# A dense mixture of experts, worked row by row only for the chosen experts, in two halves of the tokens

## The reference

```python
x = _layernorm(x + attention(x))        # 16 heads of 128, causal
x = _layernorm(x + _L0_ffn_ref(x))      # 32 experts of width 96, top 6 by sigmoid, shared width 192
x = _layernorm(x + _L1_attn_ref(x))     # a state space model (SSM), 8 heads, causal convolution, gated
x = _layernorm(x + _L1_ffn_ref(x))      # 16 experts of width 176 in 4 groups (2 groups, then top 4), shared width 352
```

## Time and profile before

| what | value |
|---|---|
| time, median of 3 runs | 1664.05 us (1663.39 to 1666.93) |
| profiled execution: its own time and its span | 1664.1 us, the same, as the time counts from the first to the last instruction |
| instructions | 29632 |
| PE busy | 1607.4 us, 97% |
| DVE, ACT, POOL busy | 1131.1, 764.6, 628.7 us |
| DMA moved | 277.75 MB, mean 167 GB/s |

### The profile page before, as it was taken

How to read it: one execution, slowest core, us unless ns; L and a number is a source line. 1 busy time by engine, 2 the same in 40 slices (tenths; PEclk the granted TensorE clock), 3 DMA queues, 4 the chain that set the end, 5 groups by cost and what they waited for, 6 DMA issues and landing times.

```text
span 1664.1 us, 29632 instructions
## 1 busy us (share of the span) xinstructions
PE 1607.4 (97%) x9944; PEld 1403.7 (84%) x9944; DVE 1131.1 (68%) x2877; ACT 764.6 (46%) x1889; POOL 628.7 (38%) x379
## 2 busy tenths in 40 slices
PE   7999999999999979999999999999999999999997
PEld 6988888898888868888888888888888888888886
DVE  5878878787887765556467568748784867753533
ACT  5666656666665543434433443325333533323221
POOL 2322223232222004323377335841575147533242
PEclk9999999999999999999999999999999999999999
DMA  6444335343443016666676556655655466555563
GB/s 212 159 140 143 141 118 180 132 158 139 142 141 137 1 59 205 191 196 205 199 225 188 184 176 209 194 187 165 207 189 175 146 206 197 178 175 172 195 206 107
DMA packets 101241, 277.75 MB, mean 167 GB/s; under 512 B 13488, under 2 KB 17584, under 8 KB 100112
## 3 DMA queue, kind: packets, MB, share of 16 engines
q1 hardware_dynamic: 101136, 276.39, 51.6%
HBM read 229.18 MB, written 46.63 MB: 166 GB/s over the span
## 4 chain that ended last, share of the span: by engine, by line
PE 60%; issue 14%; DVE 13%; POOL 6%; ACT 4%; DMA 1%; SPq 1%; POOLq 0%; DVEq 0%; ACTq 0%
PE psum L352 54%; POOL act_sb L578 4%; PE psum L1324 2%; DVE s_sb L1019 1%; PE psum L1335 1%; PE psum L1514 1%; POOL mix L600 1%; ACT p_sb L701 1%; PE psum L1314 1%; ACT kT_hi L660 1%; DVE s_sb L1017 1%; DVE kT_lo L913 1%; DVE pT_lo L1034 1%; DVE x L934 1%; DVE p_sb L1027 1%
## 5 line engine op out<-in xcount | busy, mean ns | idle before, releaser
L352 PE MATMUL psum<-xT_hi,gu_w 128*128 128x512 f32 x1616 | 550.3, 401 | 4.2 <-DVE act_sb L1082 4.0
L578 POOL TENSOR_TENSOR act_sb<-act_sb,comb 128x512 f32<-128x512 f32 x184 | 311.1, 1691 | 614.8 <-DVE act_sb L1082 614.6
L1082 DVE TENSOR_TENSOR act_sb<-psum,gated 128x512 f32<-128x512 f32 x204 | 140.7, 690 | 378.9 <-PE psum L352 372.6
L742 ACT ACTIVATE gated<-psum 128x512 f32<-128x512 f32 x204 | 122.2, 599 | 600.3 <-PE psum L352 597.8
L352 PEld LDWEIGHTS psum<-xT_hi,gu_w 128*128 128x128 f32 x1616 | 304.2, 188 | 78.0 <-DVE act_sb L1082 5.6
L352 PE MATMUL psum<-xT_lo,gu_w 128*128 128x512 f32 x808 | 319.6, 395 | 0.0
L352 PEld LDWEIGHTS psum<-d_w,act_hi 128*128 128x128 f32 x1632 | 221.5, 188 | 19.7 <-issue 2.1
L544 POOL TENSOR_TENSOR split_stage<-raw_stage,split_stage 128x768 fp32r<-128x768 f32 x56 | 103.1, 1840 | 354.2 <-ACT split_stage L650 354.2
L352 PE MATMUL psum<-d_w,act_hi 128*128 128x256 f32 x1632 | 227.7, 282 | 0.4 <-ACT act_hi L750 0.4
L352 PEld LDWEIGHTS psum<-xT_lo,gu_w 128*128 128x128 f32 x808 | 152.2, 188 | 28.8
L1088 DVE TENSOR_TENSOR act_lo<-act_sb,act_hi 128x512 fp32r<-128x512 f32 x204 | 148.8, 729 | 2.1 <-ACT act_hi L750 1.8
(11 more groups left out here) (203 smaller groups left out, 3473.6 us busy)
## 6 DMA issues: line engine op xcount, KB each, us to landing
gu_w<-w_split SPq DMA_DIRECT2D x204, 512.0 KB, 3.6
d_w<-w_split SPq DMA_DIRECT2D x204, 256.0 KB, 3.8
w_split<-split_stage SPq DMA_DIRECT2D x56, 768.0 KB, 3.9
raw_stage<-w_all SPq DMA_DIRECT2D x56, 384.0 KB, 4.3
decay_all<-decay_dram SPq DMA_DIRECT2D x32, 384.0 KB, 5.3
in_w<-w_split SPq DMA_DIRECT2D x40, 256.0 KB, 4.1
aw_raw<-attn_w SPq DMA_DIRECT2D x8, 1024.0 KB, 6.3
comb<-l_comb_dram SPq DMA_DIRECT2D x128, 64.0 KB, 3.1
```

The source lines that it names most:

```text
L352: last = nc.tensor.matmul(out_ap, w, m, start=start and n == 0, stop=stop and n == len(pairs) - 1, **kw)
L578: pool.tensor_tensor(act_sb[:, s % 2, :], act_sb[:, s % 2, :], comb[:, comb_block(s) % 2, :], ALU.mult).then_inc(comb_done, 1)
L742: act.activation(gated[to, s % 2, :], psum[0:to.stop - to.start, G_BANK, :], ACT.Silu).then_inc(gated_ready, 1)
L1082: dve.tensor_tensor(act_sb[r, s % 2, :], psum[r, G_BANK if packed(s) else U_BANK, :], gated[r, s % 2, :], ALU.mult).then_inc(t_ready, 1)
```

## The change

Attention stays as it is, without the splitting of weights for later layers. In its place SP zeroes two areas in DRAM (`xs`, one for each half of the tokens, 42 stores).

The feed-forward layers work only chosen rows. Tokens are taken in two halves of 1024. After the norm, DVE chooses experts per token (`choose`), and a place is made for each (token, chosen expert): PE counts with a triangular matrix (`rank`), DVE makes row numbers (`slots`), and POOL scatters each token's row to them, one indirect DMA of 128 rows for each tile and choice (`scatter`). Every expert has its own region of 1024 rows in `xs`. A block is 128 consecutive rows of one region. The number of blocks is fixed by the worst case: 79 per half in the first layer, 47 in the second. `table` makes, on DVE, the first row of each block; SP reads it into registers (8 at a time) and loads the block's weights and rows by it (`block_load`). PE turns the rows (`block_turn`), makes gate and up and down (`block_gate_up`, `block_down`), ACT does the silu, DVE the product (`block_act`), ACT copies the result out, SP stores it. POOL gathers for each token its 6 or 4 result rows (`gather`), and DVE adds them to x with their weights (`combine`). All of this, the shared blocks and the SSM are multiplied in plain fp32, one matmul for a product, no split.

The stream (`STREAM`) has 316 blocks: 16 shared blocks of the first layer (two for each tile of 128 tokens, half 0), 79 chosen of half 0 with the 16 shared ones of half 1 placed in pairs after each 8, 79 chosen of half 1, then in the second layer 16 shared and 47 chosen for each half. The SSM's parts for half 0 are spread over the blocks of the first layer's half 1 (90 slots over 79 blocks), those for half 1 over the second layer's shared and chosen blocks of half 0 (90 slots over 63). `slots_at` gives the slots behind a block. The second layer's half 1 and the last gathers have no SSM beside them.

```diff
-L0 = dict(layer=0, experts=32, width=96, shared=192, top=6, rows=32, reuse=3)
-L1 = dict(layer=1, experts=16, width=176, shared=352, top=4, groups=4, top_groups=2, rows=16, reuse=11)
+HALVES = 2
+HALF_TILES = TILES // HALVES
+HALF_T = T // HALVES
+BLOCK = 128
+L0 = dict(layer=0, experts=32, width=96, top=6, up=2 * 96)
+L1 = dict(layer=1, experts=16, width=176, top=4, groups=4, top_groups=2, up=3 * P)
...
+def most_blocks(f):
+
+    return (HALF_T * f["top"] + f["experts"] * (BLOCK - 1)) // BLOCK
...
+BETWEEN = 8
+STREAM = shared_blocks(L0, range(HALF_TILES))
+FIRST = {}
+for _f, _h in ((L0, 0), (L0, 1), (L1, 0), (L1, 1)):
+    if _f is L1:
+        FIRST["shared", _h] = len(STREAM)
+        STREAM += shared_blocks(L1, range(HALF_TILES * _h, HALF_TILES * (_h + 1)))
+    FIRST[_f["layer"], _h] = len(STREAM)
+    for _m, _b in enumerate(routed_blocks(_f, _h)):
+        STREAM.append(_b)
+        if (_f, _h) == (L0, 0) and _m % BETWEEN == BETWEEN - 1 and _m < HALF_TILES * BETWEEN:
+            STREAM += shared_blocks(L0, [HALF_TILES + _m // BETWEEN])
...
+XB_RING, OUT_RING = 4, 4
+L1_RING = 4
+L0_RING = 2 * L1_RING
...
+FRONT = 8, 40
+SLOTS = 90
+SPAN = (FIRST[0, 1], FIRST["shared", 0]), (FIRST["shared", 0], FIRST["shared", 1])
+
+
+def slots_at(n):
+
+    for h, (a, b) in enumerate(SPAN):
+        if a <= n < b:
+            for v in range((n - a) * SLOTS // (b - a), (n - a + 1) * SLOTS // (b - a)):
+                yield h, v
...
+            def block_load(n):
+                f, h, m, _ = STREAM[n]
+                r = ROUTED_OF[n]
+                row = first_row_of(n)
+                k, turn = ring_of(r)
+                if r < L0_ROUTED:
+                    if r >= L0_RING:
+                        sp.wait_ge(b_down_done, ROUTED[r - L0_RING] + 1)
+                else:
+                    sp.wait_ge(b_down_done, ROUTED[max(r - L1_RING, L0_ROUTED - 1)] + 1)
...
+            for n in range(-4, BLOCKS + 1):
+                for lead, f in ((4, L0), (3, L1)):
+                    if 0 <= n + lead < BLOCKS and is_routed(n + lead) and STREAM[n + lead][0] is f:
+                        block_load(n + lead)
+                if n >= 1 and is_routed(n - 1):
+                    block_store(n - 1)
...
+            def scatter(f, q):
...
+                for t in range(QUAD * q, QUAD * (q + 1)):
+                    for k in range(f["top"]):
+                        pool.indirect_dma_start(xs[q // 2], bass.IndirectOffsetOnAxis(ap=row_of[:, t, k:k + 1], axis=0), x[:, t, :], None) \
+                            .then_inc(scattered[q], 16)
...
+            def combine(f, t):
...
+                dve.wait_ge(og_loaded[i % MIX_RING], 16 * gathered(f, t))
+                for k in range(f["top"]):
+                    ins = dve.scalar_tensor_tensor(x[:, t, :], og[:, i % MIX_RING, k, :], mix_of[f["layer"]][:, t, k:k + 1], x[:, t, :], ALU.mult, ALU.add)
...
             def project(p, k):
-                n, part = IN_JOBS * p + k, slice(p * PT, (p + 1) * PT)
-                pe.wait_ge(in_loaded[n % IN_RING], 16 * (n // IN_RING) + 16)
-                pairs = []
-                for c in range(DC):
-                    w = slice(c * P, (c + 1) * P)
-                    pairs += passes(in_w[:, n % IN_RING, 0, w], in_w[:, n % IN_RING, 1, w], xT_hi[:, c, part], xT_lo[:, c, part])
-                chain(psum[:, proj_bank(k), :], pairs).then_inc(proj_ready, 1)
+                part = slice(p * PT, (p + 1) * PT)
+                chain(psum[:, proj_bank(k), :], [(in_w[:, k, c, :], xT[:, c, part]) for c in range(DC)]).then_inc(proj_ready, 1)
...
+            block_gate_up(0)
+            for n in range(BLOCKS):
+                if n + 2 < BLOCKS and is_routed(n + 2):
+                    block_turn(n + 2)
+                if n + 1 < BLOCKS:
+                    block_gate_up(n + 1)
+                block_down(n)
```

More of the change, by code:

```diff
@@ new lines, with out_place, ring_of @@
+L0_ROUTED = HALVES * L0["blocks"]
+XB_RING, OUT_RING = 4, 4
+L1_RING = 4
+L0_RING = 2 * L1_RING
+def out_place(n):
+    f, h, m, _ = STREAM[n]
+    before = sum(-(-STREAM[FIRST[k]][0]["blocks"] // 2) for k in ((0, 0), (0, 1), (1, 0), (1, 1)) if FIRST[k] < FIRST[f["layer"], h])
+    return before + m // 2, m % 2
+def ring_of(r):
+    if r < L0_ROUTED:
+        return r % L0_RING, r // L0_RING
+    r -= L0_ROUTED
+    k = r % L1_RING
+    return k, len(range(k, L0_ROUTED, L0_RING)) + r // L1_RING
@@ new lines, in gathered @@
+def gathered(f, t):
+    return sum(LAYERS[i]["top"] for i in range(2) for u in range(TILES)
+               if (i, u) <= (f["layer"], t) and (i * TILES + u) % 2 == (f["layer"] * TILES + t) % 2)
+FRONT = 8, 40
[6 more added lines that the diff above has]
+                yield h, v
```

1483 lines of the change are left out of this document (734 added, 749 removed).

## The result

The changed kernel took 1996.82 us (1992.68 to 2003.11, 4 runs) against 1663.80 (1663.39 to 1666.93) for the one before on the same chip: ratio 1.199 [1.197, 1.202]. The forecast was 1740 (1590 to 1870): the sign was right, the size much too small. Later, beside other kernels, the same unedited kernel took 2011 and 1995, but once 1867.5 (ratio 1.120 [1.117, 1.122]). So 129 us of the 257 by which the forecast was short come and go from one set of runs to another, and 128 are always there. Both need a cause.

The account below looks back on a forecast made before the run. PE was taken as the bound, busy 97% of the span. Attention 612, then the start, four feed-forward stages and tail summed to 1714; on 1102 us, the accounting's 3% shortfall added 30: about 1740 us, range 1590 to 1870.

Parts of the forecast that it names:

- Start of the stream: After attention (612): 48 POOL scatters 1.0 us apart from about 600 to 650, first chosen block at 655, bounds 636 and 690.
- second rival: Scatters and gathers: POOL's DMAs take 1.7 us, lengthening start, both span starts, second-pair products and tail; 1870 us, chance 0.12.
- First layer, half 0: 79 chosen and 16 shared blocks: PE 148 us, DVE's weight bursts +25, loads hardly above PE's pace; 176 us, to 831.
- The two stages with the SSM: First layer half 1 takes 291 us, to 1122; second layer half 0 takes 327, to 1449.
- Larger-of sum: SSM stages: each block costs the larger of PE's and DVE's time, summed block by block: 277 and 295 us.
- 6 us a tile against a slot of 3: Start of first layer's half 1: sums wait for six gathers a tile, 6 us against a slot of 3; +14 us.
- Second layer, half 1: Last stage without SSM: 16 shared blocks at 2.8 and 47 chosen at 3.6 us; 214 us, to 1663.
- worst case of 5.3 us: Last stage, down product to a block's loaded rows: issues 0.9, transfer 2.3, latency 2.1; 5.3 us against a PE block of 2.52.
- Tail: After the last block: 32 gathers of 1.0 with their sums, the norm 5.6, the store; 51 us, bounds 25 and 70.
- third rival: Last stage and start: the clock falls to 1.2 GHz where PE idles in each block; about 1825 us, chance 0.08.
- prices of PE: Unsplit products: 128 columns 0.23 us, 256 columns 0.46; a chosen block 1.60 in the first layer, 2.52 in the second.
- PE busy behind 612: After attention: PE has 784 us of work, blocks 608 and SSM 176, in place of about 1040.

Follow-up runs that it names:

- set 0: The changed kernel, unedited, four runs on one chip beside the kernel before: 1996.82 us against 1663.80, ratio 1.199.
- set 5: On one chip, four runs each: the changed kernel unedited, 1867.51 us, and the changed kernel without its 160 scatters and 160 gathers, 1721 us.
- set 1: Edits of the changed kernel, each run once: without scatters 1797 us, without gathers 1776, scatters issued one by one 2025, without scatters and gathers 1733.
- rows first: Changed kernel with chosen blocks' rows loaded ahead of their weights, except a half's first: 1942 us; again 1936.25 against 1995.27 unedited.

## Why the prediction was wrong, step by step

The forecast's stages beside the unedited kernel with late signals (set 0), without them (set 5), and without any indirect DMA (set 5), in us:

| stage | forecast | late | not late | neither |
|---|---|---|---|---|
| first chosen block | 655 | 765 | 675 | 658 |
| first layer, half 0 | 176 | 192 | 194 | 192 |
| half 1 with SSM | 291 | 329 | 317 | 269 |
| second layer, half 0 | 327 | 383 | 368 | 327 |
| half 1 | 214 | 269 | 259 | 235 |
| tail | 51 | 63 | 62 | 36 |
| sum | 1714 | 2001 | 1876 | 1717 |

(Of the first row, the runs' figure is the first chosen block's gated product; its turning stands at 762, 670 and 654.) The forecast's sum is within 3 us of the last column. That is a warning: it had indirect DMAs in it at some 100 us (21 at the start, 14, 32, and 32 in the tail), and came out like the kernel that has none, because the other terms were as much too small: that agreement is luck. Against set 0 the sum is short by 110 us at the start, 16, 38, 56 and 55 in the four stages and 12 in the tail; against set 5 by 20, 18, 26, 41, 45 and 11. What failed most is the start (late signals, point 1), the stages with the SSM (work held behind gathers and scatters, point 3) and the 3.6 us a block of the last stage (point 4).

**1. "Start of the stream": a POOL DMA 1.0 apart, first chosen block at 655.** Without late signals it stands at 675. The scatters' line (count, ns min/median/max, first and last start) and two of them in the timeline, set 0:

```profile
L622 POOL DMA_INDIRECT xs<-x,row_of x160: 956/960/2513, 602.4 to 1683.3; - x160
```

```profile
632.92 0.96 POOL L622 DMA_INDIRECT xs<-x,row_of  x1 [0.30 <-issue]
634.18 0.96 POOL L622 DMA_INDIRECT xs<-x,row_of  x1 [0.30 <-issue]
```

0.96 us of work, and 0.30 before the next, 1.26 apart: 48 of them 60 us instead of 48. Yet without any scatter the block isn't at 634, as the forecast's terms give (612, and 22 for the shared blocks), but at 658: the 16 shared blocks take 40 us, with the choice's code between them. So the scatters' share, 17 us, was nearly right (21), and PE's cover was taken as bare blocks. With late signals it is 765: the forecast put PE's signals to ACT and DVE at no time at all, and 90 of the 126 us between the two traces are lost here. The second rival had POOL's DMAs at 1.7; it priced the wrong thing, but its place was right.

The Trainium skill, "SBUF — State Buffer" (SBUF: two separate sides), had been put beside that rival: a DMA of 0.62 us issued from POOL takes 3.1 while DVE holds the shared port. In the row above the longest of 160 scatters took 2.51; here it is, beside a scan of DVE's:

```profile
1184.25 2.51 POOL L622 DMA_INDIRECT xs<-x,row_of  x1 [0.30 <-issue]
1184.25 1.74 DVE L1234 TENSOR_TENSOR_SCAN mix<-decay_all,start_row 128x768 f32<-128x768 f32 x1
```

Of both kinds together 12 of 320 took over 1.2 us, and 11 of these 12 end 0.75 to 0.79 us behind the end of such a scan. So the trace agrees in kind, and it is 11 us, no cause of the miss.

**2. "First layer, half 0": 176.** 192 to 194 in all three columns, so not the indirect DMAs. PE was busy 161 us, against 148, at a granted clock of 0.92.

**3. The two stages with the SSM: 291 and 327.** "Larger-of sum" plus gathers. Without indirect DMAs they took 269 and 327, where the sum less its terms for gathers and scatters was 277 and 295. With them they cost 48 and 41 more, where 14 and 32 were set. Against set 5, set 1 has 29 and 23 less in these stages without gathers, and 14 and 31 less without scatters. The step that failed is what a gather and a run of scatters block. From the trace without late signals, ACT, DVE and PE at the start of the first SSM stage:

```profile
904.93 0.27 ACT L794 ACTIVATE b_gated<-psum 96x128 f32<-96x128 f32 x1 [1.16 <-PE psum L411]
...
909.26 3.11 DVE L1099 SCALAR_TENSOR_TENSOR x<-og,l_mix_of,x 128x256 f32<-128x256 f32 x6 [6.60 <-DMA og<-l_os,l_back_of]
...
912.40 0.29 DVE L1115 TENSOR_TENSOR b_act<-psum,b_gated 96x128 f32<-96x128 f32 x1
...
912.74 1.22 PE L411 MATMUL psum<-bw,b_act 96*128 96x256 f32 x2 [7.84 <-DVE b_act L1115]
```

DVE takes its work in order. It waits 6.6 us for a tile's gathers and adds for 3.1, and the gated product, whose input ACT had ready at 905.20, stands behind both until 912.40; PE, only a block ahead, waits 7.84. Over the kernel DVE waits thus 77.3 us in 14 places. The forecast had this wait (6 us a tile against a slot of 3), but only at the start.

The scatters do the same on POOL. The next layer's scatters stand in front of POOL's products for the second pair, and PE waits for these:

```profile
1106.97 1.19 PE L1554 MATMUL psum<-mix,h_tok 128*128 128x256 f32 x2 [16.06 <-POOL mix L652]
```

A second such wait, in the second layer, is 12.4 us. In all PE waits 29.7 us for these products in set 5 and as much without gathers, 4.6 without scatters, and has no such wait with neither kind. The forecast had a term for it in the second layer's half 0 only, and put it at nothing in the first layer's half 1.

**4. "Second layer, half 1": 16x2.8+47x3.6.** Measured 16x3.4 (54 us) and 47x4.36 (205) without late signals. The mechanism named, rows that come late because of the order on SP and the weights' buffers, is shown by the runs with rows first. The worst case of 5.3 us from down product to turned rows was right too: 5.6 on average in set 5. What failed is the term made of it, 3.6 a block. The wait comes once in two blocks, and PE's work behind the turning (3.4) comes on top: (5.6+3.4)/2 = 4.5. The forecast softened 5.3 towards 2.52 for four buffers of rows, which don't bear on it. Without any indirect DMA the stage took 235, 24 less; how they lengthen it isn't shown. The Trainium skill, "DMA: Bandwidth & Descriptors" (Two DMAs through the same engine are not ordered), says that descriptors within a queue of one DMA engine start in order and are pipelined. No run here shows how much that holds the rows up: they landed 4.4 us behind their issue after the weights and 5.0 ahead of them.

**5. "Tail": 51.** 63 with and 62 without late signals, 36 without gathers. 32 gathers at 1.25 are 40 us; the forecast's 1.0 makes the other 8.

**6. The clock.** The third rival gave 0.08 to a fall to 1.2 GHz, in the last stage and the start. The granted clock is 0.84 to 0.86 in three of the four long stages above, and 0.58 and 0.53 in the first and last. A block's six unsplit products (12 records), twice in the last stage of set 0:

```profile
1851.20 1.50 PE L411 MATMUL psum<-xbT,bw 128*128 128x128 f32 x12
...
1855.75 2.16 PE L411 MATMUL psum<-xbT,bw 128*128 128x128 f32 x12
```

The second took 2.16 in place of 1.50, at a granted clock of 0.66 in 1855.7 to 1857.9 against 1.00 in 1851.2 to 1852.7, so part of it at the lower level (1.2 GHz), behind a wait of 1.71 us for rows. The prices of PE themselves were right: at full clock a first-layer block takes 1.58 from turning to turning (957.80 to 959.38, 1.60 forecast). PE busy behind 612 was to be 784. It is 950 in set 0, 935 in set 5 and 894 without indirect DMAs, 110 to 166 us more for the same work. Not all of that is the clock: a matmul's row is longer than its distance to the next (0.44 against 0.28 for the two turnings at 957.80), and the difference counts as busy at each of the 116 to 125 waits of PE, an estimated 20 us. How much of the rest lies on the path is argued, not shown: no experiment kept the clock up. It can explain the first layer's half 0, the same 16 to 18 us too long with and without indirect DMAs, and part of the 32 in the second layer's half 0, since PE sets the pace there between its waits.

**What held.** PE's share fell to 76% (about 80% said); PE waits for xb in the last stage and for b_act in the SSM stages; the second rival's figure of 1870 is near 1867.5, by other terms. Attention ended as forecast: the first shared block's gated product stands at 620 without late signals. With them it stands at 670, and these 50 us are part of the 90 at the start. Of the signs that were named, 1.0 from scatter to scatter (1.26), 655 for the first chosen block and 3.6 in the last stage didn't hold.

## What to carry to other kernels

Before a chain of indirect DMAs is put beside a dense stream, ask which in-order engine waits for each of them, and what ready work stands behind that wait: of 158 us that the indirect DMAs cost in the traces of set 5, 44 lie at the start and in the tail, where nothing covers their own time, and 89 in the two stages with the SSM. Where an engine runs only one block ahead, don't let the load that is needed first stand behind a wait that guards another load's buffer; to move it ahead was worth 3%. When experiments are spread over several runs, carry the unedited kernel along in each: two theories here, on kinds and on number of DMAs, rested on nothing but comparing across them.

## What the hardware showed unexpectedly

- In some sets PE's finished work was noticed by ACT and DVE up to 27 us late while POOL issued indirect DMAs; 3 sets of 6 with 9 kernels had it, 3 with 10 hadn't, and one chip had a set of each kind. It cost 128 us of 1995 (1995.27 against 1867.51, in two sets). SP's issues of loads in that stretch stood 3.5 to 5.7 us apart (0.5 to 0.9 from 667 to 674 in set 5). The kernel before showed no sign of it in its time. The cause is open.
- An indirect DMA begun beside a scan of DVE's (768 columns, 1.74 us or more) ended 0.75 to 0.79 us behind it, in 11 cases, and took up to 2.51 us instead of 0.96.
- An indirect DMA of 128 rows of 1 KB took POOL 0.96 us and 0.30 to the next, and landed 2.4 us (scatter) and 2.8 us (gather) behind its issue, in the median.
- 12 us (0.7%) lay between two sets for the kernel without indirect DMAs (1733 and 1721), more than a set's own spread tells.
